# Storing each output strip of a four-layer convolution as eight transfers of one image row in place of one transfer

## The chip, the cores and the metric

One Trainium2 chip, one of its cores. The metric is the device time of one execution in microseconds (us), lower is better. The kernel before took 5070.35 us, the median of two runs (5067.87 and 5072.84).

## What is computed

The input `x` is float32, 8 images of 16 channels of 512 by 512. Four layers follow one another, each adding a function of the group-normalised input (`_gn`, 8 groups of 2 channels):

```python
# layer 0: 3x3 convolution of the spectrum, complex weights and bias
x = x + _L0_conv_ref(_gn(x), w_real, w_imag, b_real, b_imag)
# layer 1: channels split in halves u and v, each row kept or zeroed by the sign of a dot product
x = x + _L1_conv_ref(_gn(x))
# layers 2 and 3: real 3x3 convolutions, padding 1, 16 to 16 channels
x = x + _L2_conv_ref(_gn(x), L2_conv_W)
x = x + _L3_conv_ref(_gn(x), L3_conv_weight)
return x                      # (8, 16, 512, 512), float32
```

## The kernel before, in words

An image is held on the chip as 64 strips (`STRIPS`). A strip is 8 image rows (`ROWS`) of all 16 channels: 128 partitions (partition = 16 times the row within the strip, plus the channel) by 512 columns, 256 KB. Two strips make a pair (`PAIRS` = 32). The images run one after the other: for each image first the mixing stage (layers 0 and 1; TensorE lines L1109 to L1133), then layer 2 and then layer 3 (both TensorE line L1201, in 32 by 32 tiles of the array). While image i is in its mixing stage, the strips of image i+1 are loaded and summed as well; while it is in layer 3, TensorE and ScalarE also prepare constants of image i+1.

No planner orders the work: each engine has its instructions written out in a fixed order, and semaphores tie the engines together. `more` is true for all images but the last.

**Sync engine (SP).** All DMA transfers are issued here, in line. After the constants (L352) and the first pass over image 0 (L383 to L387, one load of x and one of a table per strip) it runs `image(i, more)`, L392. That issues the x and table loads of pairs 1 and 2 (`load_pair`, L366), then per pair the loads of the next image (`load_next`, L376) and of the pair three ahead, then pair 0 of the next image (L410), and then the stores of layer 3: a loop of 8 turns with 8 strips each (L412 to L415). Each store waits until ScalarE has evicted its strip (`evicted`) and increments the semaphore `c_stored[k]` of its slot by 16. The loads of pairs 1 and 2 of the next image stand behind the last of these stores. At the end the engine waits until all slots' stores have landed (L422).

**ScalarE (ACT).** In layer 3 `evict3` (L580) copies each finished strip out of PSUM into one of eight slots of 512 columns (`cout`, a part of the tile `shared`); the odd strips of a pair take two activations of 64 partitions. Before it writes a slot it waits at L585 until the store that read the slot last has landed: `i * STORES + use * 16`, where `STORES` counts the increments of a slot per image.

**TensorE (PE).** In layer 3 a pair uses two of six PSUM banks, and pair n waits until pair n-3 has been evicted (`first3`).

**VectorE (DVE).** The slots share their memory with `planes`, the products that the mixing stage of the next image needs. So DVE waits in `slots_stored` (L775) for slots 0 to 3 before it makes the planes of strips 0 and 1, and for slots 4 to 7 before those of pair 1; then `make_planes` (L751) waits for x and works on `xin` and `planes` (L757 to L767), and `copy_v` (L769) takes TensorE's mixture out of PSUM. `slots_stored` compares with `i * STORES`.

GpSimd has no part in this.

Of the kernel before, what the change touches and what calls it, by code (L numbers as in the profile page):

```python
# [12 lines left out]
B, C, N = 8, 16, 512  # L13
P = 128
HP = P // 2
ROWS = 8
# [9 lines left out]
GROUP = 4  # L26
GROUPS = STRIPS // GROUP
SLOTS3 = 2 * GROUP
STORES = 16 * GROUPS // 2
WIDE = N + 2  # L30
PAIRS = STRIPS // 2
DEPTH2, LAG2 = 4, TAPS + 1
# [9 lines left out]
FREE = 1  # L42
# [150 lines left out]
def program(nc, x, t_eye, t_hil, t_fix, t_trig, t_strip, t_rows, t_gsel, t_zsel, t_fold, t_partner, t_eye_mix,  # L193
            t_eye_conv, t_small, t_bias, w_mix, w_u, w_bias, w_conv, out):
    with ExitStack() as ctx:
# [3 lines left out]
        def sem(name):  # L199
            return ctx.enter_context(nc.semaphore(name))  # L200
# [51 lines left out]
        cout = shared[:, 0:SLOTS3 * N].rearrange("p (k w) -> p k w", w=N)  # L252
# [49 lines left out]
        c_stored = [sem(f"out_stored{k}") for k in range(SLOTS3)]  # L302
# [11 lines left out]
        def v1(k, p0=0, p1=P):  # L314
            return vec[p0:p1, k:k + 1]
# [24 lines left out]
        def ev(i, n):  # L340

            return i * EVICTED + n + FREE

        @block.sync
        def _(sp):
            for dst, src in ((eye[:], t_eye), (hil[:], t_hil), (fix[:], t_fix), (trig[:], t_trig),
                             (gsel[:], t_gsel), (zsel[:], t_zsel), (fold[:], t_fold), (conv_w[:], w_conv), (conv_eye[:], t_eye_conv), (partner[:], t_partner),
                             (small[:], t_small), (bias_w[:], w_bias), (eye_mix[:], t_eye_mix), (row_trig[:], t_rows),
                             (x1f[:, 0:576], w_mix.rearrange("p a b c d -> p (a b c d)")),
                             (x1f[0:ZR, 1536:1824], w_u.rearrange("p a b c d -> p (a b c d)")),  # L350
                             (x1f[:, 2048:3072].rearrange("p (a b) -> p a b", a=2), t_bias)):
                sp.dma_start(dst, src).then_inc(s_const, 16)  # L352

            def load_x(i, s, pair, k):

                sp.wait_ge(mixed, i * PAIRS + pair - 1 + MIXED_CREDIT)
                if type(s) is int:
                    sp.sem_inc(s_sp, 1)
                sp.dma_start(xin[:, k % UNROLL, :], x[i].rearrange("c (s r) w -> s r c w", r=ROWS)[s]).then_inc(x_loaded[k % UNROLL], 16)

            def load_table(i, s, pair, k):

                sp.wait_ge(h_done, i * STRIPS + pair * 2 - 5 + H_CREDIT)
                sp.dma_start(strip[:, k, :], t_strip[s]).then_inc(tab_loaded[k], 16)

            def load_pair(i, pair, slot):  # L366

                for e in range(2):
                    load_x(i, pair * 2 + e, pair, slot + e)
                for e in range(2):  # L370
                    load_table(i, pair * 2 + e, pair, slot + e)

            for k in range(SLOTS3):
                sp.sem_inc(c_stored[k], FREE)

            def load_next(image, s, t, k):  # L376


                sp.wait_ge(a_squared, t + 1)
                sp.wait_ge(a_projected, t + 1)  # L380
                sp.dma_start(xa[:, k, :], x[image].rearrange("c (s r) w -> s r c w", r=ROWS)[s]).then_inc(a_loaded[k], 16)  # L381

            with sp.Fori(0, STRIPS // UNROLL) as j:  # L383
                for k in range(UNROLL):
                    s = j * UNROLL + k
                    load_next(0, s, s, k)
                    sp.dma_start(strip[:, k, :], t_strip[s]).then_inc(a_table[k], 16)  # L387

            sp.wait_ge(a_projected, STRIPS + A_CREDIT)
            load_pair(0, 0, 0)  # L390

            def image(i, more):  # L392

                def feed(pair, slot):

                    if more:
                        for e in range(2):
                            load_next(i + 1, pair * 2 + e, i * STRIPS + pair * 2 + e + STRIPS, (slot + e) % UNROLL)
                    if type(pair) is not int or pair + AHEAD < PAIRS:
                        load_pair(i, pair + AHEAD, (slot + 2 * AHEAD) % TABLES)  # L400

                for pair in range(1, AHEAD):
                    load_pair(i, pair, 2 * pair)
                with sp.Fori(0, PAIRS // UNROLL - 1) as j:
                    for k in range(UNROLL):
                        feed(j * UNROLL + k, 2 * k)
                for pair in range(PAIRS - UNROLL, PAIRS):
                    feed(pair, 2 * pair % TABLES)
                if more:
                    load_pair(i + 1, 0, 0)  # L410

                with sp.Fori(0, GROUPS // 2) as j:  # L412
                    for k in range(SLOTS3):
                        sp.wait_ge(evicted, ev(i, 1 + STRIPS + j * SLOTS3 + k + 1))
                        sp.dma_start(out[i].rearrange("c (s r) w -> s r c w", r=ROWS)[j * SLOTS3 + k], cout[:, k, :]).then_inc(c_stored[k], 16)  # L415

            with sp.Fori(0, B - 1) as i:
                image(i, True)
            image(B - 1, False)

            for k in range(SLOTS3):
                sp.wait_ge(c_stored[k], B * STORES + FREE)  # L422

# [11 lines left out]
        def _(act):  # L435
# [66 lines left out]
            def image(i, more):  # L502
# [77 lines left out]
                def evict3(n, banks, e, use):  # L580

                    for k in range(2):
                        o = e * 2 + k
                        act.wait_ge(convolved, i * CONVOLVED + 1 + PAIRS + n + 1)
                        act.wait_ge(c_stored[o], i * STORES + use * 16 + FREE)  # L585
                        for h in range(1 + k):
                            to, of = (slice(0, P), slice(0, P)) if k == 0 else (slice(HP * h, HP * h + HP), slice(HP - HP * h, P - HP * h))
                            ins = nc.scalar.activation(cout[to, o, :], ps[of, banks[k], :], ACT.Identity, bias=v1(BIAS3, to.start, to.stop))  # L588
                        ins.then_inc(evicted, 1)
# [9 lines left out]
                for n in range(PAIRS):  # L599
                    if more and n == C_AT[0]:  # L600
                        keep_parts(i + 1)
                    if more and n == C_AT[1]:
                        keep_turned(i + 1)
                    if more and n == C_AT[2]:
                        keep_sums(i + 1)
                    evict3(n, banks3(n), n % SLOT_PAIRS, n // SLOT_PAIRS)
# [6 lines left out]
        def _(dve):  # L613
# [130 lines left out]
            def image(i, more):  # L744
# [30 lines left out]
                def slots_stored(first, n):  # L775

                    for k in range(first, first + n):
                        dve.wait_ge(c_stored[k], i * STORES + FREE)
                        dve.sem_inc(s_dve, 1)
# [523 lines left out]
```

## Time and profile before

| | |
|---|---|
| median of the runs | 5070.35 us |
| the profiled execution | 5067.6 us |
| its span | 5065.8 us |
| mean granted TensorE clock | 0.955 |
| TensorE matmuls busy | 4614.4 us, 91% |
| TensorE weight loads busy | 2945.6 us, 58% |
| VectorE busy | 2926.5 us, 58% |
| ScalarE busy | 2499.3 us, 49% |
| DMA | 471.79 MB, mean 93 GB/s |

The span runs from the first to the last instruction of the profiled execution. Matmuls are pipelined and their ends are modelled, so a busy TensorE isn't one at its peak. Instructions that issue a DMA aren't counted as busy; the sync engine's own are listed under the name SPq, and PEld is TensorE's weight load. L415 is line 415 of the kernel before. Images take about 610 us each after a first stage of some 160 us.

### The profile page before, as it was taken

What the parts mean: (1) busy time and instruction counts of PE and PEld (TensorE: products, weight loads), DVE (VectorE), ACT (ScalarE), POOL (GpSimd) and SP (SyncE); (2) the same over time, 40 slices, a digit from 0 to 9 for tenths busy, and PEclk for the clock granted to TensorE, in tenths of its full rate; (3) what the DMA queues carried; (4) which work ended last, traced back from release to release, by engine and by line L of the source; (5) the groups of instructions that cost most, each with busy time, mean ns of one, the idle gap of its engine ahead of it and who ended that gap; (6) DMA issues with size and microseconds to landing.
All of it is one profiled execution on the core that took longest, in us unless ns stands there. A gap on an engine that the chain in (4) does not pass through costs nothing.

```text
span 5065.8 us, 222775 instructions
## 1 busy us (share of the span) xinstructions
PE 4614.4 (91%) x84784; PEld 2945.6 (58%) x84784; DVE 2926.5 (58%) x10596; ACT 2499.3 (49%) x7097; POOL 3.2 (0%) x14
## 2 busy tenths in 40 slices
PE   3699898998989999998989989899898998988888
PEld 0365665566655566565656556556565566655566
DVE  0377734777157671776617765277643777257670
ACT  4355445553445535454445544455444554444435
POOL 0000000000000000000000000000000000000000
PEclk9899999998999999998999989999899999999999
DMA  5344024440344304442044411444024440232104
GB/s 166 92 125 123 25 68 139 124 121 5 93 135 123 103 3 125 127 126 75 14 141 126 122 54 40 137 126 123 31 62 135 125 122 13 89 100 74 52 3 136
DMA packets 294845, 471.79 MB, mean 93 GB/s; under 512 B 22288, under 2 KB 97104, under 8 KB 294224
## 3 DMA queue, kind: packets, MB, share of 16 engines
q1 hardware_dynamic: 294224, 462.41, 30.3%
q8 instruction: 524, 8.59, 0.7%
q14 instruction: 97, 0.79, 0.0%
HBM read 328.10 MB, written 134.22 MB: 91 GB/s over the span
## 4 chain that ended last, share of the span: by engine, by line
PE 88%; DVE 4%; issue 3%; DMA 2%; SPq 1%; ACT 1%; ACTq 0%; DVEq 0%
PE ps L1201 33%; PE ps L1124 18%; PE ps L1109 17%; PE ps L1117 5%; PE ps L985 5%; PE ps L1133 4%; DMA shared<-t_strip 1%; PE ps L1226 1%; PE ps L1015 1%; PE ps L1177 1%; PE ps L1029 0%; SPq L381 0%; PE ps L980 0%; PE ps L1030 0%; DMA out<-shared 0%
## 5 line engine op out<-in xcount | busy, mean ns | idle before, releaser
L1201 PE MATMUL ps<-x,conv_s 32*32 32x512 f32 x49104 | 1720.8, 602 | 32.8 <-issue 32.7
L1201 PEld LDWEIGHTS ps<-x,conv_s 32*32 32x32 f32 x49104 | 1231.3, 103 | 490.0 <-issue 248.3
L1124 PE MATMUL ps<-hil,shared 128*128 128x256 f32 x4096 | 993.6, 386 | 0.0
L520 ACT ACTIVATE x<-ps,vec 128x256 f32 (+1 forms) x1024 | 490.6, 495 | 998.9 <-PE ps L1124 998.9
L1124 PEld LDWEIGHTS ps<-hil,shared 128*128 128x128 f32 x4096 | 740.4, 190 | 273.8 <-issue 194.1
L761 DVE SCALAR_TENSOR_TENSOR shared<-xin,trig 128x256 f32<-128x256 f32 x2048 | 812.0, 434 | 57.4
L588 ACT ACTIVATE shared<-ps,vec 64x512 f32<-64x512 f32 (+1 forms) x768 | 525.7, 685 | 442.7 <-PE ps L1201 432.2
L773 DVE COPY vsb<-ps 128x512 f32<-128x512 f32 x512 | 329.9, 686 | 583.6 <-PE ps L1109 583.6
L1109 PE MATMUL ps<-shared 32*32 32x512 f32 x16384 | 665.0, 613 | 0.0
L757 DVE TENSOR_SCALAR xin<-xin,vec 128x512 f32<-128x512 f32 x512 | 245.6, 480 | 655.3 <-DMA out<-shared 623.9
L577 ACT ACTIVATE x<-ps,vec 128x512 f32 x512 | 347.7, 685 | 462.4 <-PE ps L1201 462.4
L1109 PEld LDWEIGHTS ps<-shared 32*32 32x32 f32 x16384 | 312.2, 104 | 284.2 <-issue 221.9
L915 DVE TENSOR_SCALAR x<-x,cols,gate_b x1024 | 361.6, 449 | 80.2 <-issue 68.6
L985 PE MATMUL ps<-shared 128*64 128x512 f32 x1024 | 304.8, 675 | 99.7 <-DMA shared<-t_strip 99.7
L1109 PE MATMUL ps<-xin,shared 32*32 32x512 f32 x8192 | 307.4, 623 | 96.5 <-DVE shared L761 57.5
L925 DVE SCALAR_TENSOR_TENSOR work<-x 128x512 f32 (+1 forms) x512 | 332.3, 708 | 96.7 <-ACT x L577 96.6
L443 ACT ACTIVATE shared<-shared 128x512 f32<-128x512 f32 x512 | 322.3, 630 | 119.6 <-DMA shared<-x 45.6
L788 DVE SCALAR_TENSOR_TENSOR work<-x,colv 128x512 f32<-128x512 f32 x512 | 333.9, 687 | 61.5 <-ACT x L520 61.5
L1133 PEld LDWEIGHTS ps<-eye,vsb 128*128 128x128 f32 x2048 | 316.7, 202 | 58.5 <-DVE vsb L773 20.9
L531 ACT ACTIVATE shared<-x 128x512 f32 (+1 forms) x512 | 326.8, 638 | 46.0 <-ACT shared L531 44.5
L1133 PE MATMUL ps<-eye,vsb 128*128 128x128 f32 x2048 | 325.6, 282 | 19.5 <-DVE vsb L773 12.2
L513 ACT ACTIVATE shared<-ps 128x384 f32<-128x384 f32 x512 | 249.6, 487 | 104.7 <-PE ps L1133 91.9
(161 smaller groups left out, 2676.7 us busy)
## 6 DMA issues: line engine op xcount, KB each, us to landing
shared<-x SPq DMA_DIRECT2D x512, 256.0 KB
xin<-x SPq DMA_DIRECT2D x512, 256.0 KB
out<-shared SPq DMA_DIRECT2D x512, 256.0 KB
shared<-t_strip SPq DMA_DIRECT2D x576, 96.0 KB, 3.4
hil<-t_hil SPq DMA_DIRECT2D x1, 560.0 KB, 3.4
trig<-t_trig SPq DMA_DIRECT2D x1, 512.0 KB, 4.6
x<-t_bias SPq DMA_DIRECT2D x1, 512.0 KB, 5.0
x<-w_mix SPq DMA_DIRECT2D x1, 288.0 KB, 3.3
```

The costliest lines, as they stand in the source:

```text
L520: ins = nc.scalar.activation(split_in(strip_of(s))[:, q, :], split_in(ps[:, bank, :])[:, q, :], ACT.Identity, bias=v1(MEAN), accum_out=sum ...
L577: nc.scalar.activation(strip_of(s), ps[:, banks[k], :], ACT.Identity, bias=v1(MEANP), accum_out=cols[:, 2, bass.ds(s, 1)]).then_inc(evicte ...
L588: ins = nc.scalar.activation(cout[to, o, :], ps[of, banks[k], :], ACT.Identity, bias=v1(BIAS3, to.start, to.stop))
L761: ins = V.scalar_tensor_tensor(halves_in(planes[:, a, k, :], q), halves_in(xin[:, k, :], q), 1.0, trig_of(a, q), ALU.mult, ALU.mult, accum ...
L788: V.scalar_tensor_tensor((vc, vy)[odd], strip_of(s), 1.0, colv, ALU.mult, ALU.mult, accum_out=cols[:, 2, bass.ds(s, 1)]).then_inc(dotted, 1)
L915: ins = V.tensor_scalar(of, of, cols[:, 4, bass.ds(s, 1)], gate_b[:, q, bass.ds(s, 1)], ALU.mult, ALU.add)
L925: V.scalar_tensor_tensor((vc, vs)[k % 2], strip_of(s), 1.0, strip_of(s), ALU.mult, ALU.mult, accum_out=red[:, k:k + 1]).then_inc(c_squared, 1)
L985: mm = pe.matmul(ps[HP * e:HP * (e + 1), BZ, :], strip[:, t + e, P:P + HP], xa[:, k + e, :], start=first, stop=False, skip_group_check=True)
L1109: mm = pe.matmul(ps[TM * cg:TM * cg + TM, bank, :], wst[TM * rg:TM * rg + TM, k, v, a, :], of[TM * rg:TM * rg + TM, :], start=(a == AXS), ...
L1124: mm = pe.matmul(split_in(ps[:, BY + 2 * odd + e, :])[:, int(q < 2), :], xt[:, e, q, :], hil[:, q, 0:HALF], start=False, stop=True, skip_g ...
L1133: mm = pe.transpose(ps[:, BX, q * P:(q + 1) * P], chunk(q)(vsb[:, e, :]), eye[:])
L1201: mm = pe.matmul(ps[TM * cg:TM * cg + TM, banks[k], :], conv_s[TM * rg:TM * rg + TM, kw, second, :], x1[TM * rg:TM * rg + TM, of, kw:kw + ...
```

## The change

Each strip of 128 partitions is stored by eight transfers, one for each image row: 16 partitions (the channels) by 512 columns, 32 KB. All eight increment the slot's semaphore by 16, so a stored strip now counts 128 (`STRIP_STORE`), and the thresholds of ScalarE, DVE and of the end, which go by `STORES`, follow.

```diff
-STORES = 16 * GROUPS // 2
+STRIP_STORE = 16 * ROWS
+STORES = STRIP_STORE * GROUPS // 2
...
                     for k in range(SLOTS3):
                         sp.wait_ge(evicted, ev(i, 1 + STRIPS + j * SLOTS3 + k + 1))
-                        sp.dma_start(out[i].rearrange("c (s r) w -> s r c w", r=ROWS)[j * SLOTS3 + k], cout[:, k, :]).then_inc(c_stored[k], 16)
+                        for r in range(ROWS):
+                            sp.dma_start(out[i].rearrange("c (s r) w -> s r c w", r=ROWS)[j * SLOTS3 + k, r],
+                                         cout[C * r:C * r + C, k, :]).then_inc(c_stored[k], 16)
...
-                        act.wait_ge(c_stored[o], i * STORES + use * 16 + FREE)
+                        act.wait_ge(c_stored[o], i * STORES + use * STRIP_STORE + FREE)
```

## Rows read from the trace of the kernel before

**Rows 1.** Page: chain that ended last, and the costliest group of instructions.

```profile
PE 88%; DVE 4%; issue 3%; DMA 2%; SPq 1%; ACT 1%; ACTq 0%; DVEq 0%
...
L1201 PE MATMUL ps<-x,conv_s 32*32 32x512 f32 x49104 | 1720.8, 602 | 32.8 <-issue 32.7
```

**Rows 2.** Busy time by stretch: engines' us, PEclk, DMA share, GB/s.

```profile
800.00:810.00 10.00, 6.96 (x182) 4.24 (x160) 0.00 (x0) 6.58 (x10) 0.00 (x0) 1.00 0.51 170
810.00:820.00 10.00, 4.27 (x81) 2.02 (x96) 7.75 (x33) 0.00 (x0) 0.00 (x0) 0.53 0.43 150
```

**Rows 3.** Waits from 690 to 810 us: us in total, times, longest.

```profile
ACT shared L588 <- PE ps L1201: 54.1, 31, 6.8
```

**Rows 4.** Sync engine's timeline, stores of the eight images, next load: start, us.

```profile
692.18 117.77 SPq L415 DMA_DIRECT2D out<-shared  x64
810.91 1.77 SPq L359 DMA_DIRECT2D xin<-x  x2
...
1303.39 121.84 SPq L415 DMA_DIRECT2D out<-shared  x64
...
1914.44 115.78 SPq L415 DMA_DIRECT2D out<-shared  x64
...
2522.24 117.33 SPq L415 DMA_DIRECT2D out<-shared  x64
...
3129.89 119.10 SPq L415 DMA_DIRECT2D out<-shared  x64
...
3740.68 122.41 SPq L415 DMA_DIRECT2D out<-shared  x64
...
4351.74 114.69 SPq L415 DMA_DIRECT2D out<-shared  x64
...
4955.91 105.04 SPq L415 DMA_DIRECT2D out<-shared  x64
```

**Rows 5.** Instructions of line L415: duration ns min/median/max, first and last start.

```profile
L415 SPq FUSED_REGOPS  x512: 52/103/103, 692.0 to 5060.2; - x171
L415 SPq MOVE out<-shared x512: 29/29/36, 692.1 to 5060.3; - x171
L415 SPq DMA_DIRECT2D out<-shared x512: 606/611/720, 692.2 to 5060.3; - x171
```

**Rows 6.** Sync engine's timeline in the first pass over image 0.

```profile
13.08 0.62 SPq L381 DMA_DIRECT2D shared<-x  x1
13.90 0.34 SPq L387 DMA_DIRECT2D shared<-t_strip  x1
14.55 0.62 SPq L381 DMA_DIRECT2D shared<-x  x1
```

**Rows 7.** Sync engine's timeline at the start, two of the constants.

```profile
1.21 0.41 SPq L352 DMA_DIRECT2D hil<-t_hil  x1
...
5.45 0.64 SPq L352 DMA_DIRECT2D small<-t_small  x1
```

**Rows 8.** Instructions of the table load's line L387.

```profile
L387 SPq FUSED_REGOPS  x64: 37/42/42, 10.7 to 155.6; - x64
```

**Rows 9.** Page: DMA packets of the whole span.

```profile
DMA packets 294845, 471.79 MB, mean 93 GB/s; under 512 B 22288, under 2 KB 97104, under 8 KB 294224
```

**Rows 10.** Turn to image 1: chain piece, timeline, and VectorE's wait.

```profile
803.65 6.09 DMA out<-shared
...
816.59 0.49 DVE L757 TENSOR_SCALAR xin<-xin,vec 128x512 f32<-128x512 f32 x1 [1.31 <-DMA xin<-x]
...
819.16 0.08 DVE L761 DVE_READ_ACCUMULATOR shared<-xin,trig 128x1 f32 x1
...
822.67 0.48 DVE L757 TENSOR_SCALAR xin<-xin,vec 128x512 f32<-128x512 f32 x1
...
825.75 1.17 PE L1109 MATMUL ps<-xin,shared 32*32 32x512 f32 x16 [0.96 <-DVE shared L761]
...
DVE xin L757 <- DMA out<-shared: 623.9, 7, 91.6
```

**Rows 11.** DMA issues: KB each, median us from issue to landing.

```profile
shared<-t_strip SPq DMA_DIRECT2D x576, 96.0 KB, 3.4
...
small<-t_small SPq DMA_DIRECT2D x1, 1.0 KB, 3.8
```

## The prediction

> **What bounds the kernel now.** First the chain of work that ended last and the groups of instructions: the chain is TensorE for 88%, a third of the span its line L1201, the two 3x3 convolutions [rows 1]. Then busy time by stretch of the first image's layer 3 and of the turn to the next image: TensorE is busy 6.96 of 10 us as layer 3 closes and 4.27 of the next 10, where its granted clock is 0.53, so about its lower level [rows 2]. Then who waits for whom in layer 3: ScalarE (the evictions, L588) waits 54.1 us, and for TensorE; no wait for a free output slot is listed [rows 3]. So layer 3 is paced by TensorE, and the stores follow it.
>
> Last the sync engine's own timeline, since all that the change adds is issued there. Its 64 stores of an image take 117.77 us in the first image and 105.04 in the last; the eight stretches add up to 933.96 us, 116.7 each, or 1.82 us a strip [rows 4]. Of these 1.82 us the engine spends 0.611 issuing [rows 5]; the rest it waits for evictions. That spare 1.2 us a strip is what the change may use free of charge.
>
> **What the change removes.** Per strip one issue of 256 KB. **What it adds:** eight issues of 32 KB each, all in line on the same queue. The bytes, the evictions and the eight output slots stay. ScalarE's wait for a slot now wants 128 in place of 16, the same condition in substance. The strip's slot is free when its eighth row has landed.
>
> **Price of one row issue.** No row shows a store of 16 partitions. The nearest rows:
> - A store now: 0.611 us of issue [rows 5]. An x load with the same image-side pattern (8 rows, 16 channels, 512 columns): 0.62; a table load with a plain two-dimensional pattern: 0.34 [rows 6]. Constants issued once: 0.41 for 560 KB, 0.64 for 1 KB [rows 7]. So the duration follows neither the bytes nor, visibly, the partitions; an eighth of the bytes doesn't make an eighth of the issue.
> - Around it the address registers: from the end of an x issue to the start of a table issue 0.20 us (13.08 + 0.62 to 13.90), no wait between [rows 6], of which the table's register operations are 0.08: 0.042 for its fused one [rows 8], nearly as much for its move. A store has 0.103 + 0.029 = 0.13 [rows 5]. So 0.12 of fixed gap + 0.13 = 0.25.
> The kind of the issue is the choice. A row store is two-dimensional, channels by columns, like the table; and it goes over all 16 DMA engines, like the table, where the present store goes over 8. This the packets show: 22,288 are under 512 B [rows 9]. The short ones are one completion packet per engine and transfer, and the short rows of four constants (128 each, 512). 1536 image transfers by 8 + 576 tables by 16 + 17 constants by 16 + 512 = 22,288 to the packet, where 16 engines everywhere would give 34,576. The Trainium skill says how that comes about (DMA: Bandwidth & Descriptors, "Why a DMA increments its semaphore by 16 and not by 1": the engine count divides the slowest dimension of both sides, 8 for this store, 16 for a channel row, and with fewer than 16 the issuing sequencer writes the rest of the semaphore itself); the trace agrees with the count. I take 0.34 + 0.25 = **0.59 us** a row. Ends: below, 0.34 + 0.10 = 0.44, if most of the address work is hoisted; above, the full price of a store, 0.61 + 0.25 = 0.86.
>
> **Per strip:** 8 x 0.59 = 4.72, and once the wait for the eviction and the loop's share, 0.13 (a register operation and the wait; the gap ahead of an x issue with waits is 0.31 against 0.25, [rows 6], doubled for what I can't see): 4.85 us against 1.82. The spare 1.2 us is used up by the third row. So the queue becomes the bound of layer 3: ScalarE fills eight slots, then waits for landed stores, TensorE behind it for free banks.
>
> **Per image:** SyncE also issues the next image's loads of pairs 1 and 2 behind the stores (810.91 in the first image), so nothing after layer 3 can make the time good: x of pair 1 lands 5.7 us after that issue (DVE takes it at 816.59) and TensorE mixes pair 1 at 825.75 [rows 4, 10]. Everything later hangs on the end of the stores. They take 64 x 4.85 = 310.4 us in place of 116.7, +193.7; for eight images 2483 - 934 = **+1549 us**.
>
> **What goes the other way.** At the turn the first four slots are free 4 strips (19 us) before the stores end. DVE's planes of pair 0, and TensorE's mix of it, which now start when the stores end (the chain piece of 6.09 us from 803.65 is the store that DVE waits for, [rows 10]), are done early. Of the 14.8 us from 810.91 to 825.75 there remain 5.7 for the load, 2.65 for one set of planes (816.59 to 819.24), 1.3 for the two copies out of PSUM that stand behind it in program order, and 3.1 from the other set's start, 822.67, to TensorE: 12.75 [rows 10]. Gain 2 us at 7 turns, 14, and an estimated 1 us at the turns and at the end from last transfers that are smaller: -20 us in round figures. TensorE's clock: with 3 us of work per pair in every 9.7 us it may fall to the lower level, where the pair takes 6 us, still hidden. It enters the next image low, as it does now [rows 2]; at most some 5 us a turn, 35 in all, left to the range. DVE and GpSimd issue nothing in the changed stretch; the next image's preparation on TensorE and ScalarE sits inside layer 3 and has more cover than before.
>
> **Sum:** 5067.6 (the profiled execution, 1.8 above its span and 2.75 under the median of the runs) + 1549 - 20 = 6597; I say 6595.
>
> **Can the DMA engines keep up?** In the last 10 us of layer 3 the 16 engines are busy 0.51, which for a store on 8 engines is nearly all of them, at 170 GB/s [rows 2]. A row store takes 0.59 us of issue for 32 KB, 56 GB/s. From these, a 2 KB packet takes 8.2 engines / 83 packets per us = 0.10 us; each engine has one per row, and a completion packet of unknown price. The constants were issued 0.47 apart (nine steps from 1.21 to 5.45, [rows 7]) and still landed in 4 us or so (3.8 for the 1 KB one, [rows 11]), so completions to SBUF pipeline; for image memory no row shows it.
>
> **Rivals.**
> - *Full price.* The row issue costs like a store, 0.86 us, because the cost lies in the output side (its strides or its two loop registers): 8 x 0.86 + 0.13 = 7.01 a strip, 3589 for eight images, +2655 - 20: **7700 us**. For it: x loads and stores both cost 0.62, tables alone 0.34. Against: they share the 8 engines too.
> - *Cheap row.* Addresses hoisted, 0.44: 3.65 a strip, 1869, +935 - 20: **5980 us**. Against: each x, table and store issue shows its own register operation.
> - *Not slower: issue shrinks with the transfer.* Place: the sync queue in layer 3. If a row issue cost an eighth of 0.611, 0.08, plus a short gap, and the whole came to no more than 1.82 / 8 = 0.228 us, TensorE would go on pacing layer 3, and 16 engines instead of 8 would empty the slots sooner: of the 6.09 us of the chain from 803.65 at most all is saved, 8 times, about -49: **5020 us**. The 0.20 gap alone nearly fills the threshold, and the 1 KB constant took 0.64. The Trainium skill leans this way (same page, "Issuing engines are not separate DMA queues": an issue's sequencer time is usually small beside the DMA itself). In the trace it is 0.611 of about 1.54 us of transfer at 170 GB/s, not small once the transfer is cut in eight.
> - *The engines pace it.* Each row holds its engines as long as a whole store does, about 1.5 us (completion into image memory not pipelined): 12 us a strip, 6144, **10,260 us**. The completion packet can't be that dear now: 16 packets of 0.10 fill the 1.54 us.
>
> **Chances.** Forecast 0.62 (row issue 0.54 to 0.68, so 4.45 to 5.57 a strip: 6390 to 6965), full price 0.18, cheap 0.12, not slower 0.04, engines 0.04. The range takes in the cheap and the full price: 5980 to 7700. A difference of 2%, 101 us, is about what a measurement here can tell from none; faster 0.02, within it 0.02, slower 0.96.
>
> **What the changed profile would show.** 4096 store issues of about 0.34 us, 0.59 apart, in eight unbroken stretches of about 310 us; ScalarE at the evictions of layer 3 waiting for stores; the chain with some 37% on the sync queue; about 55 GB/s in layer 3; under-512-B packets 22,288 - 4096 + 65,536 = 83,728; layers 0 to 2 as long as before. DVE's wait of 623.9 / 7 = 89 us before the first planes [rows 10] would grow by 175 or so (the stretch's 194 less the four early strips). **Wrong** if issues come under 0.23 apart, if the engines and not the issues fill the stretch, or if the next image doesn't move with the end of the stores.

## The result and the profile after

The change makes the kernel slower: 6483.16 us (median of 6477.84 and 6488.47) against 5070.35 us, a ratio of 1.279 with a 95% interval of 1.2737 to 1.2843. The profiled execution took 6488.47 us.

The page of the changed kernel shows it as a whole: span and busy times, the clock, packets, and the chain that ended last (it answers to [rows 1] and [rows 9]).

```profile
span 6486.7 us, 233527 instructions
PE 4967.0 (77%) x84784; PEld 2923.4 (45%) x84784; DVE 2925.5 (45%) x10596; ACT 2496.2 (38%) x7097; POOL 3.2 (0%) x14
...
DMA packets 356324, 472.35 MB, mean 73 GB/s; under 512 B 83728, under 2 KB 158544, under 8 KB 355664
...
PE 56%; SPq 28%; issue 11%; DVE 3%; DMA 2%; ACT 1%; ACTq 0%; DVEq 0%
SPq L417 26%; PE ps L1127 14%; PE ps L1204 14%; PE ps L1112 13%; PE ps L1120 4%; PE ps L988 4%; PE ps L1136 4%; DMA shared<-t_strip 1%; SPq L415 1%; PE ps L1229 1%; PE ps L1018 0%; DMA xin<-x 0%; PE ps L1180 0%; SPq L382 0%; PE ps L983 0%
```

TensorE's share falls from 91% to 77%; a quarter of the chain now runs through the sync engine's store line, L417. The packets under 512 B are the 83,728 of the prediction, so a row store does go over 16 engines. TensorE's busy time grew (4614.4 to 4967.0 us) at a lower granted clock (0.867 in the mean of the span, 0.955 before); that cost nothing, as shown below.

The instructions of the row store's line in the changed kernel (duration in ns, min/median/max) answer to [rows 5]:

```profile
L417 SPq FUSED_REGOPS  x4096: 37/37/108, 693.9 to 6484.5; - x196
L417 SPq MOVE out<-shared x4096: 29/29/29, 694.0 to 6484.6; - x196
L417 SPq DMA_DIRECT2D out<-shared x4096: 314/315/1946, 694.1 to 6484.6; - x196
```

The issue is 0.315 us in the median, and the register operation 0.037 instead of 0.103. The register operation takes up to 0.108 ahead of the first row of a strip. Some issues took up to 1.946 us; the longest of the kernel before, on any line, took 1.055.

The sync engine's timeline, first image (start, us; it answers to [rows 4]):

```profile
694.07 294.72 SPq L417 DMA_DIRECT2D out<-shared  x512
992.81 2.60 SPq L360 DMA_DIRECT2D xin<-x  x2
```

One unbroken stretch of 294.7 us in place of 117.8. The eight stretches add up to 2352.8 us against 933.96: +1418.8, and the span grew by 1420.9. The seven turns from one image's last store to the next image's first add up to 3438.1 against 3434.8. **So the whole loss lies between the first and the last store of each image.**

A piece of the chain of waits inside the stretch (start, us, what) shows how it is filled:

```profile
978.21 0.32 SPq L417
978.52 0.04 issue
978.71 0.32 SPq L417
979.02 0.04 issue
979.20 0.31 SPq L417
979.52 0.04 issue
979.56 0.10 SPq L415
979.66 0.04 issue
979.70 0.11 SPq L417
979.91 0.32 SPq L417
...
983.40 1.18 SPq L417
```

From row to row 0.50 us (978.21, 978.71, 979.20); from the last row of a strip to the first of the next 0.71 (979.20 to 979.91), as the wait and a longer register operation stand between. And then an issue of 1.18 us.

Who waits from 700 to 980 us (us in total, times, longest), to be held against [rows 3]; and busy time, granted clock, DMA share and GB/s of a stretch inside:

```profile
DVE xin L760 <- DMA out<-shared: 251.1, 1, 251.1
ACT shared L591 <- DMA out<-shared: 183.4, 53, 4.7
...
PE ps L1204 <- ACT shared L591: 78.1, 20, 5.9
```

```profile
900.00:950.00 50.00, 24.95 (x432) 10.01 (x432) 0.00 (x0) 11.61 (x17) 0.00 (x0) 0.68 0.26 59
```

The waits have turned round: ScalarE waits for stores to land, and TensorE for ScalarE. TensorE is busy half of the time at a granted clock of 0.68, and still waits. The DMA engines are busy 0.26 at 59 GB/s; before, 0.51 at 170 [rows 2].

### The profile page after: what moved, and what is told of

It reads as the page before. It is cut to its first block, busy times and chain, and to the rows that moved or that the text cites. A ratio compares the mean times of both kernels' runs of the same rounds, so it can differ in the third digit from the quotient of the medians.

```text
span 6486.7 us, 233527 instructions
## 1 busy us (share of the span) xinstructions
PE 4967.0 (77%) x84784; PEld 2923.4 (45%) x84784; DVE 2925.5 (45%) x10596; ACT 2496.2 (38%) x7097; POOL 3.2 (0%) x14
## 2 busy tenths in 40 slices
DMA packets 356324, 472.35 MB, mean 73 GB/s; under 512 B 83728, under 2 KB 158544, under 8 KB 355664
## 4 chain that ended last, share of the span: by engine, by line
PE 56%; SPq 28%; issue 11%; DVE 3%; DMA 2%; ACT 1%; ACTq 0%; DVEq 0%
SPq L417 26%; PE ps L1127 14%; PE ps L1204 14%; PE ps L1112 13%; PE ps L1120 4%; PE ps L988 4%; PE ps L1136 4%; DMA shared<-t_strip 1%; SPq L415 1%; PE ps L1229 1%; PE ps L1018 0%; DMA xin<-x 0%; PE ps L1180 0%; SPq L382 0%; PE ps L983 0%
## 5 line engine op out<-in xcount | busy, mean ns | idle before, releaser
L1204 PE MATMUL ps<-x,conv_s 32*32 32x512 f32 x49104 | 2037.4, 704 | 653.0 <-ACT shared L591 652.2
L1204 PEld LDWEIGHTS ps<-x,conv_s 32*32 32x32 f32 x49104 | 1190.1, 112 | 1471.6 <-issue 1271.3
L591 ACT ACTIVATE shared<-ps,vec 64x512 f32<-64x512 f32 (+1 forms) x768 | 524.9, 683 | 1611.6 <-DMA out<-shared 1482.5
L760 DVE TENSOR_SCALAR xin<-xin,vec 128x512 f32<-128x512 f32 x512 | 246.1, 481 | 1901.1 <-DMA out<-shared 1761.0
```

The costliest lines, as they stand in the source:

```text
L1204: mm = pe.matmul(ps[TM * cg:TM * cg + TM, banks[k], :], conv_s[TM * rg:TM * rg + TM, kw, second, :], x1[TM * rg:TM * rg + TM, of, kw:kw + ...
```

## The experiments

The theory, called Q, is that the sync queue's issues pace layer 3. Its rivals: the DMA engines do (E); each strip pays as a whole; the issues of all queues share one generator. A time without an interval is that of a single execution. The intervals are those of the ratio to the kernel before, measured again beside each group of runs (medians 5069.58 to 5073.93 us).

**Little data in the same issues.**

```diff
-[j * SLOTS3 + k, r], cout[C * r:C * r + C, k, :]
+[j * SLOTS3 + k, r, :, 0:N // 8], cout[C * r:C * r + C, k, 0:N // 8]
```

> All eight row stores of a strip are issued, but each carries 64 of the 512 columns (seven eighths of the output are left out). Theory Q, the sync queue's issues pace layer 3: the eight stretches of stores stay at about 294 us each (2353 us in all) and the time near 6480 us; at least 6300, if the issues over 0.8 us come from the bytes under way and vanish. Rival E, the DMA engines pace it: with an eighth of the bytes a strip's stores take under 1.8 us and the time returns to about 5070 us.

Measured 6489.14 us. The timeline of this kernel, first image; its median from issue to landing; and the stretch of 50 us that was shown above (last columns: granted clock, DMA share, GB/s):

```profile
692.84 298.39 SPq L417 DMA_DIRECT2D out<-shared  x512
...
out<-shared SPq DMA_DIRECT2D x4096, 4.0 KB, 1.3
...
900.00:950.00 50.00, 24.14 (x447) 9.90 (x432) 0.00 (x0) 10.65 (x16) 0.00 (x0) 0.73 0.06 9
```

An eighth of the bytes makes no difference, and the DMA engines are busy 0.06 of this stretch in place of 0.26: they are out as a cause, by their data rate and by their packets. The long issues stay too (215), so the stores' own bytes don't cause them.

**Fewer issues.**

```diff
-STRIP_STORE = 16 * ROWS
+STORED = 3        # and 4
+STRIP_STORE = 16 * STORED
...
-for r in range(ROWS):
+for r in range(STORED):
```

> Only rows 0 to 2 of each strip are stored (five eighths of the output are left out). Theory Q: 3 x 0.50 + 0.21 for the strip's wait = 1.71 us, with the long issues some 1.85, against the 1.82 us that a strip takes now: the time is that of the kernel before, 5070 to 5110 us. If instead each strip pays its price as a whole (4.60 us, the landing of its last row), the time stays near 6480.

> Only rows 0 to 3 of each strip are stored (half of the output is left out). Theory Q: 4 x 0.50 + 0.21 = 2.21 us a strip, with the long issues 2.4, so 154 us per image in place of 116.7: +300, about 5370 us (5250 to 5400). Rival E, half the bytes over 16 engines, 128 KB in under 0.8 us: 5070 us.

Measured 5195.25 us with three rows (1.0243, interval 1.0225 to 1.0260) and 5462.72 with four (1.0758, 1.0740 to 1.0776). Both are above what was expected, 5110 and 5400 at most. The first stretch of stores with three rows, and with four:

```profile
690.27 135.94 SPq L418 DMA_DIRECT2D out<-shared  x192
```

```profile
692.26 169.84 SPq L418 DMA_DIRECT2D out<-shared  x256
```

From three rows to four the time grows by 267 us, 512 strips of 0.52; from four to eight by 1020, or 255 per row. So the cost is close to a straight line in the number of issues, with an offset that doesn't shrink: the issues over 0.15 us above the median number 207, 204 and 219 with three, four and eight rows, and their excess is 168, 183 and 180 us, 21 to 23 us per image. I had made that excess proportional to the issues. With 0.50 n + 0.21 + 0.35 us a strip, n = 3, 4 and 8 give 2.06, 2.56 and 4.56; measured were 2.12, 2.65 and 4.60 in the first image. Three rows are already over the 1.82 us of [rows 4].

**What an issue's price hangs on: two 8-channel transfers for row 7.**

```diff
-for r in range(ROWS):
-    sp.dma_start(out...[j * SLOTS3 + k, r], cout[C * r:C * r + C, k, :])
+for r in range(ROWS):
+    for c, n in ((0, C),) if r < ROWS - 1 else ((0, C // 2), (C // 2, C // 2)):
+        sp.dma_start(out...[j * SLOTS3 + k, r, c:c + n], cout[C * r + c:C * r + c + n, k, :])
```

> Row 7 of each strip is stored in two transfers of 8 channels, which go over 8 engines but are as two-dimensional as the others: nine issues a strip. If the 0.31 us against 0.61 us of an issue hangs on the number of engines (8 instead of 16), these two take 0.6 each: +1.1 us a strip, +560, about 7040 us. If it hangs on the number of dimensions, they take 0.31: +0.5 us a strip, +256, about 6740 us.

Measured 6667.47 us, 73 under the second value: the two short issues save some 34 of it, and only 163 issues are long here, with an excess of 135 us in place of 180. The issues of 8 channels took 0.28 us in the median, less than those of 16 channels (0.315). So 8 engines are not what makes an issue dear.

**Three dimensions, channels outermost: pairs and fours of strips.**

```diff
-for k in range(SLOTS3):
-    sp.wait_ge(evicted, ev(i, 1 + STRIPS + j * SLOTS3 + k + 1))
+for k in range(0, SLOTS3, TOGETHER):            # TOGETHER = 2 or 4
+    sp.wait_ge(evicted, ev(i, 1 + STRIPS + j * SLOTS3 + k + TOGETHER))
     for r in range(ROWS):
-        sp.dma_start(out[i].rearrange("c (s r) w -> s r c w", r=ROWS)[j * SLOTS3 + k, r], cout[C * r:C * r + C, k, :])
+        sp.dma_start(out[i].rearrange("c (s r) w -> r c s w", r=ROWS)[r, :, bass.ds(j * SLOTS3 + k, TOGETHER), :],
+                     cout[C * r:C * r + C, k:k + TOGETHER, :])
```

(One semaphore serves the slots of a group.)

> Stores wait for two strips, and each of eight transfers then carries one image row of both (16 channels by 2 strips by 512, 64 KB, over 16 engines): half the issues, the same bytes. The pattern has three dimensions. Theory D, an issue's 0.61 us hangs on the third dimension: 8 x (0.61 + 0.19) + 0.21 = 6.6 us a pair, 3.3 a strip and 0.35 for the long issues: 234 us per image in place of 116.7, about 6010 us. Rival K, it hung on the 8 engines and 0.31 stays: 8 x 0.50 + 0.21 = 4.2 a pair, 2.45 a strip with the long issues: 157 us, about 5390 us.

> The same with four strips (128 KB each, two issues a strip). Theory D: 8 x 0.80 + 0.21 = 6.6 us for four strips, 1.65 a strip, 2.0 with the long issues: +90 us, and up to 270 more as four slots come free together some 9 us after the fourth eviction while the other four fill in 6.5: 5160 to 5430 us. Rival K: 1.05 a strip, TensorE paces again, 5060 to 5150 us.

Measured 5430.41 us with pairs (1.0722, 1.0704 to 1.0740) and 5080.24 with fours (1.0018, 1.0008 to 1.0028). Line L419 of the kernel with pairs:

```profile
L419 SPq DMA_DIRECT2D out<-shared x2048: 315/316/2101, 693.9 to 5421.8; - x187
```

A third dimension alone costs nothing; theory D falls. With pairs the stretch is 161.3 us, 5.04 per pair or 2.52 per strip, as K expected. With fours the first stretch is back at 117.4 us:

```profile
697.68 117.39 SPq L419 DMA_DIRECT2D out<-shared  x128
```

TensorE paces again: ScalarE waits for stores only 65.8 us in the whole span, where the changed kernel has 1482.5. The image rows are still stored separately and over 16 engines (34,576 packets under 512 B, which is 22,288 - 4096 + 1024 x 16; that the prediction names the same number for 16 engines everywhere is a coincidence, the loads still go over 8), so it is the count of issues that made the loss, not the separate rows. Nor do 16 engines win anything.

**The old form, eight times.**

```diff
-for r in range(ROWS):
-    sp.dma_start(out...[j * SLOTS3 + k, r], cout[C * r:C * r + C, k, :])
+for c in range(0, N, N // 8):
+    sp.dma_start(out...[j * SLOTS3 + k, :, :, c:c + N // 8], cout[:, k, c:c + N // 8])
```

> Eight issues a strip as in the changed kernel, but each carries 64 columns of all 128 partitions, so the pattern is that of the kernel before (8 rows by 16 channels by columns on the image's side, 128 partitions on the chip's, 8 engines). If the 0.61 us of an issue hangs on this form (a 128-partition side that is split into 8 by 16) and not on its 256 KB, each costs 0.61 + 0.19: 8 x 0.80 + 0.21 + 0.35 = 7.0 us a strip, 448 us per image, about 7720 us: the rival 'full price' of the prediction. If it hangs on the size, about 6480 us.

Measured 7578.64 us. Line L417 of this kernel:

```profile
L417 SPq DMA_DIRECT2D out<-shared x4096: 606/612/1632, 691.7 to 7574.4; - x196
```

32 KB in the old form cost 0.61 us as 256 KB did. So the price follows the form, 128 partitions on one side against 8 by 16 on the other, and not the size, nor the number of engines alone, nor that of dimensions alone. Nor is it the 128 partitions alone: the table loads fill as many (128 by 768 bytes) and take 0.34 [rows 6]. Here only 39 issues are long.

**A store that is short of engines.**

```diff
-for r in range(ROWS):
-    sp.dma_start(out...[j * SLOTS3 + k, r], cout[C * r:C * r + C, k, :])
+for r in range(0, ROWS, ROWS // 2):
+    sp.dma_start(out...[j * SLOTS3 + k, r:r + ROWS // 2], cout[C * r:C * (r + ROWS // 2), k, :])
```

> Two stores a strip, each of 4 rows by 16 channels (128 KB). By the issues alone 2 x 0.80 + 0.21 + 0.35 = 2.16 us a strip at most, 138 us per image, 5070 to 5240 us. But if the number of engines is that of the outermost dimension, 4, a store's 64 packets of 0.10 us go over 4 engines: 3.2 us a strip, 205 us per image, about 5780 us: then the engines pace layer 3, which eight issues did not make them do. Packets under 512 B: 22,288 with 4 engines, as 1024 x 4 = 512 x 8.

Measured 5467.46 us, between the two. The packets, the issue line, and a stretch of layer 3 (its last columns are clock, DMA share, GB/s):

```profile
DMA packets 294846, 471.79 MB, mean 86 GB/s; under 512 B 22289, under 2 KB 97105, under 8 KB 294225
```

```profile
L417 SPq DMA_DIRECT2D out<-shared x1024: 552/934/2624, 691.6 to 5454.7; - x171
```

```profile
770.00:780.00 10.00, 6.67 (x196) 3.30 (x182) 0.00 (x0) 4.10 (x6) 0.00 (x0) 1.00 0.28 105
```

22,289 says 4 engines a store. 0.28 of 16 is 4.5 engines busy: those that are used are full, at 105 GB/s where the layer wants some 140. The stretch is 161.9 us, 2.53 a strip, 32 packets per engine of 0.079 us; I had taken 0.10. This is what an engine-bound store looks like, and it shows in the issues: the first five of a stretch take 0.56 to 0.68 us, the median of all is 0.934, so the sequencer is held up once the engines are behind. By issues of 0.56 alone a strip would take 2 x (0.56 + 0.19) + 0.21 = 1.71 us, less than TensorE's 1.82.

**Two queues.**

```diff
+ON_ACT = 3
...
-for r in range(ROWS):
+for r in range(ROWS - ON_ACT):
...
                         ins.then_inc(evicted, 1)
+                        act.wait_ge(evicted, ev(i, 1 + STRIPS + 2 * n + k + 1))
+                        for r in range(ROWS - ON_ACT, ROWS):
+                            act.dma_start(out...[2 * n + k, r], cout[C * r:C * r + C, o, :]).then_inc(c_stored[o], 16)
```

> As the changed kernel, but rows 5 to 7 of each strip are issued by ScalarE behind its own eviction, rows 0 to 4 by the sync engine. Theory Q, what limits is one queue's issuing: the sync engine needs 5 x 0.50 + 0.21 = 2.7 us a strip, 3.05 with the long issues; ScalarE a pair 2.1 of evictions and 6 x 0.5 = 5.1 us, 2.55 a strip: 195 us per image, about 5700 us (5600 to 5850). If the issues of all queues are served one after the other by a shared generator, nothing is gained: near 6480.

Measured 5729.48 us (1.1304, 1.1286 to 1.1323). The first stretch on the sync queue is 201.2 us and ScalarE's issues take 0.332 us each. The same 4096 transfers, on the same 16 engines, from two queues give back 754 us: the limit is a queue's own issuing, and not a generator that both share.

**What stands behind the stores.** In the changed kernel:

```diff
             load_pair(0, 0, 0)
+            load_pair(0, 1, 2)
...
-                for pair in range(1, AHEAD):
+                for pair in range(2, AHEAD):
...
                     load_pair(i + 1, 0, 0)
+                    load_pair(i + 1, 1, 2)
```

> As the changed kernel, but the loads of pair 1 of the next image are issued ahead of the stores instead of behind them. Theory: each turn waits at first for the loop's exit (4.05 us from the last store to the x load), then for x; with x there, DVE's planes of pair 1 wait for the last store alone: TensorE mixes pair 1 some 9 us after the last issue in place of 15, 7 times 6: -45, about 6440 us. Rival: what follows (pair 2, whose loads stay behind the stores) takes the gain back: 6480 us.

Measured 6452.43 us, 31 less than the changed kernel, of the 45 expected. From the last store to the next image's first the trace shows some 484 us in place of 491 at the seven turns, 51 us in all; the eight stretches of stores came out 2.3 us longer each, 18 in all. So the loads' place behind the stores is real and small.

**Towards a better kernel:** the same edit on the kernel before, and with stores by fours.

> The kernel before with the loads of pair 1 of the next image issued ahead of the stores. At the turn x of pair 1 is there, and DVE waits only for the last slot: 1.3 us earlier than with x at 816.59, and pair 2 is loaded earlier; 7 turns, -10 to -45 us of 5070, ratio 0.991 to 0.998. Rival: nothing, if TensorE's start at the lower clock sets the pace of the first pairs.

> Stores of one image row of four strips (eight transfers per four strips) together with the loads of pair 1 ahead of the stores. The stores alone came to a ratio of 1.002, the loads gave 31 us where the queue was the bound: 0.995 to 1.00 of the kernel before, no better than the loads alone, since 16 engines in place of 8 save nothing that TensorE waits for.

Measured 5066.11 us (0.9985, 0.9976 to 0.9994) and 5076.93 us (1.0009, 0.9999 to 1.0020). The kernel before had 5073.93 in the same session. The first lies 8 us under it, at the edge of what can be told and at the weak end of the range expected (0.991 to 0.998); the second is no faster at all and misses its range. The profile doesn't show where the 8 us come from: the seven turns add up to 3435.4 us against 3434.8.

## Why the prediction was right

- **The bound.** It said the queue takes over as the bound of layer 3 and that ScalarE and then TensorE wait. The waits have turned as said, and bytes, rows and queues were varied one at a time with the results above. The chain has 28% on the sync queue and 11% in gaps ("issue"), most of them between its instructions, where some 37% were forecast, and layer 3 moves 59 GB/s where 55 were.
- **Price of one row issue, 0.59 us.** Measured 0.50: the issue 0.315 for 0.34, and the register work 0.066 for 0.13, because the register operation is short ahead of most rows (0.037 us in the median, up to 0.108 ahead of a strip's first row). The choice "two-dimensional, like the table" was good. Its reason, that 16 engines or two dimensions make it cheap, was wrong in both halves: 8 engines took 0.28 (row 7 in two), three dimensions 0.316 (pairs). It is the form of the old store that costs 0.61 (columns). The forecast's own range for a row was 0.54 to 0.68; 0.50 lies below it.
- **Per strip, 4.85 us.** Measured 4.60: 8 x 0.50 + 0.21 + 0.35 for long issues, plus 0.05 for the loop (once in eight strips the step to the next strip is 1.08 us in place of 0.71). The two errors, too dear a row and no long issues, partly cancel, and that is luck: without the long issues the same sum gives 4.26 a strip, an estimated 6295 us, below the 6390 to 6965 that the forecast's row prices span. Of the 219 long issues 209 overlap one of the 16 KB packets on the queue that the profile calls instruction (524 over the span, about 1.04 us each in the median), which I take for fetches of code; of the 3877 other issues 131 do. Of these packets 204 fall into the eight stretches of stores, and with three and with four rows 198, so their number hardly follows the stores: this is the constant offset of those runs.
- **Per image and in all, +1549.** Measured +1418.8.
- **The third row.** "The spare 1.2 us a strip is used up by the third row": three rows cost 2.4%.
- **The other way, -20.** This step failed, at little cost: outside the stretches the span grew by 2 us. Here is the first turn of the changed kernel, to be held against [rows 10]:

```profile
972.71 0.49 DVE L760 TENSOR_SCALAR xin<-xin,vec 128x512 f32<-128x512 f32 x1 [251.09 <-DMA out<-shared]
978.37 2.02 PE L1112 MATMUL ps<-xin,shared 32*32 32x512 f32 x32 [40.31 <-DVE shared L764]
997.02 0.49 DVE L760 TENSOR_SCALAR xin<-xin,vec 128x512 f32<-128x512 f32 x1 [19.10 <-DMA xin<-x]
1000.78 0.48 DVE L760 TENSOR_SCALAR xin<-xin,vec 128x512 f32<-128x512 f32 x1
1003.87 1.17 PE L1112 MATMUL ps<-xin,shared 32*32 32x512 f32 x16 [0.40 <-DVE shared L764]
```

The mix of pair 0 is indeed done early (978.37), and from x's issue at 992.81 to pair 1 on TensorE it is 11.1 us where it was 14.8; by the next image's first store 2.3 us of it are left, in the mean of the seven turns. But from the last store's end to that issue it is 4.0 us where it was 0.95, at six of seven turns: the chain shows an idle "issue" of 3.00 us behind the loop's exit. 6 x 3.1 against 7 x 2.3, some 3 us less after the very last store, and a first store 1.9 us later: about nothing. The exit follows the length of the loop's body: with 8 or 16 issues in it (the kernel before, halves, fours) the next load came 0.9 us after the last store, with 24 to 72 (three and four rows, pairs, two queues, the changed kernel, row 7 in two) 3.1 to 4.2, at six of the seven turns each.
- **The clock.** It fell to a granted 0.68 in the mean of the stretch shown in layer 3, where TensorE was busy half of the time: the granted clock went back and forth between its two levels, 1.2 and 2.4 GHz. That cost nothing: TensorE waits for ScalarE 652 us in spite of it.
- **VectorE's wait** grew from 623.9 to 1761.0 us over 7 turns, 162 each; 175 were forecast.
- **The rivals.** Full price came true only when the old form was kept (7578.64 against 7700 forecast). Not slower would have needed 0.228 us an issue; 0.50 were measured. Engines as the bound: the run with an eighth of the bytes excludes it here. The cheap row (0.44) came nearer to the measured 0.50 than the forecast's 0.59 did, though each issue does show a register operation of its own; the long issues, 0.35 us a strip, took the time back to the forecast.

Open: why a long issue follows a code fetch. With 0.80 us between issues there were 39 long ones, with 0.50 there were 219 (163 where two of nine issues were of 8 partitions), with whole-strip stores none, though 192 such packets fell among them; that would fit a short queue ahead of the engines that a held-up engine fills, as with 4 engines, but it is only argued, and no run varied the fetches themselves. Nor is it shown what the loop's exit does in its 3 us with a long body.

## What to carry to other kernels

In this kernel the bytes were no guide and the count of issues was. Count the issues per stage and multiply by the step from issue to issue on that queue, register work and wait included (here 0.50 us, 0.80 in the costlier form); hold the product against the time the stage has, before looking at bytes. Small transfers were free while it stayed under (fours: 1.0018), and each one over cost its full step (0.50 us from four rows to eight). If a layout is wanted that needs small pieces, let one transfer span several tiles; two queues gave back only half of the loss here (1.1304 of 1.279).

## What the runs showed of the hardware

- An issue from the sync engine took 0.28 us (8 partitions), 0.315 (16), and 0.61 where 128 partitions on the chip stand against 8 rows by 16 channels in memory, whether it moved 32 or 256 KB.
- The number of DMA engines went by the outermost dimension: 4, 8 or 16, to be counted in the packets under 512 B (22,289 for two stores a strip on 4 engines, 83,728 for eight on 16).
- With row stores 209 of 219 long issues coincide with a 16 KB packet of the instruction queue, and the long ones lose 0.8 us each.
- Stores on 4 engines hold up their queue: issues of 0.56 us early in a stretch, 0.934 in the median of all.
- 32 KB stores landed 1.6 us after their issue, 64 KB 1.9, 128 KB 2.8.
